# A first score block that takes the high and low halves of K in one matmul, an output projection moved behind the third score block, and a later split of the Q weights

## The chip, the cores and the metric

The kernel runs on one core of one Trainium2 chip. A core has five engines that run side by side and wait for each other through semaphores: TensorE (PE in the profile, with its weight loads as PEld), VectorE (DVE), ScalarE (ACT), GpSimd (POOL) and SyncE (SP), which here issues the DMAs. The metric is the device time of one execution in microseconds (us); lower is better. All times below are in us unless marked ns.

## What is computed

Two transformer layers on `x` of shape (2, 512, 256), all in float32. The change lies in the attention of the second layer, which the reference writes as (cut):

```
def _L1_attn_ref(x, W_Q, W_K, W_V, W_O, b_Q, b_K, b_V, b_O):
    q = jnp.einsum('bpd,hde->bphe', x, W_Q) + b_Q
    k = jnp.einsum('bpd,hde->bphe', x, W_K) + b_K
    v = jnp.einsum('bpd,hde->bphe', x, W_V) + b_V
    scores = jnp.einsum('bqhe,bkhe->bhqk', q, k) / ATTN_SCALE
    scores = jnp.where(causal, scores, IGNORE)
    attn = jax.nn.softmax(scores, axis=-1)
    z = jnp.einsum('bkhe,bhqk->bqhe', v, attn)
    out = jnp.einsum('bqhe,hed->bqd', z, W_O) + b_O
```

There are 16 heads of 128 channels and two halves of the batch with 512 positions each, so 32 pairs of a head and a half. Ahead of it stand a first attention (3 heads) and a feed-forward part with ternary weights; behind it an int8 product.

## The kernel before

**Windows.** Each pair of a head and a half is one *window*, `w` = 0 to 31. The heads go two by two (a *pair* of heads shares one set of weights `W_hi`, `W_lo`), and a pair of heads serves four windows. The kernel is a software pipeline: while window `w` is on the engines, its instructions belong to neighbours. TensorE computes the scores of window `w+1`, the projections Q, K, V of window `w+2`, the weighted values of window `w-1` and the output projection of an older one.

**High and low parts.** Every float32 operand is split into a high part and a remainder (`Q_hi`, `Q_lo`, ...), and each product is three matmuls into the same PSUM bank: high by high, high by low, low by high (`split_mm`, lines 389 to 391). For the scores these are lines 673 to 675. ScalarE makes the high part out of PSUM, VectorE the low part.

**The order is written by hand.** For each engine there is a table of steps per window, a letter and a number each. Those that matter here:

- `S0` to `S3`: the scores of window `w+1`, query block 0 to 3 of 128 rows. Causal, so block `c` needs `128*(c+1)` keys, and its matmuls have that many columns. On VectorE `S` is `max1` (line 1435): one custom instruction adds the causal mask to the scores, writes them to `SM` and leaves the row's extreme in `nmax`. On ScalarE it is the exponential (line 924) into `PR`.
- `Q0`, `K1`, `V2`: projections of window `w+2`. They use the PSUM banks 0 and 1 in turn, so each waits until VectorE has read the one before last: `K1` waits for `V_lo` of window `w+1` (VectorE's step `W2`, line 1422), `V2` waits for `Q_lo` (VectorE's step `Q0`, line 1425), and the scores `S0` of the next window wait for `K_lo`.
- `O0`: half of an output projection, 12 matmuls of 256 columns on TensorE; on VectorE the addition of the result to `X` (line 1475). `B0`: the weighted values of window `w-1`. `Z0`: the low part of an earlier `Z`.
- `U0` to `U3`: VectorE turns the probabilities in blocks (line 1454) into `BT`; SyncE stores `BT` to DRAM and loads it back turned as `MV`; ScalarE (`C3` to `C0`, line 935) and GpSimd (`moved_low`, line 1112) split `MV` into `PT_hi` and `PT_lo`, which `B0` one window later needs. Windows 0 to 25 go this way (`by_dma`); later ones are turned by TensorE.
- `G0` to `G3`: VectorE splits the next pair's weights, when `loads_k(w)` or `loads_o(w)` say so. `G0` is `W_Q` in two instructions, `W_hi` (line 1361) and `W_lo` (line 1363); `G1` and `G2` are the high parts of `W_K` and `W_V` (line 1365), whose low parts GpSimd makes; `G3` is `W_O`. `G0` to `G2` run in windows 1, 5, 9, 13, 17, 21 and 23 only.
- `R0`, `R1`: reciprocals of the row sums; GpSimd then scales `PR` (lines 1096 to 1105).

In a window below 26 each query block has a PSUM bank of its own (`s_bank`: `bank[2 + c]`), so block 0 uses 128 of its bank's 512 columns.

Of the kernel before, what the change touches and what calls it, by code (L numbers as in the profile page):

```python
# [23 lines left out]
P = 128  # L24
# [3 lines left out]
SEQ = 512  # L28
# [32 lines left out]
def build(nc, x, wq0, wk0, wv0, fcT, fcb, wupT, wgateT, wdownT, pack1, bias_all, bo1, qw, qb, out):  # L61
    ctx = ExitStack()
    with ctx:
        def sb(name, shape, dt=F32, where=ctx):
            return where.enter_context(nc.sbuf_tensor(name, shape, dt))

        def sem(name):
            return ctx.enter_context(nc.semaphore(name))
# [9 lines left out]
        causal = sb("causal", [P, SEQ])  # L78
# [70 lines left out]

        Q_hi = sb("Q_hi", [P, 2, SEQ], F32R)  # L150
        Q_lo = sb("Q_lo", [P, 2, SEQ], F32R)
        K_hi = sb("K_hi", [P, 2, SEQ], F32R)
        K_lo = sb("K_lo", [P, 2, SEQ], F32R)
        V_hi = sb("V_hi", [P, V_GROUPS * CT, 2 * DH], F32R)
        V_lo = sb("V_lo", [P, V_GROUPS * CT, 2 * DH], F32R)
        SM = sb("SM", [P, 2, SEQ])
        PR = sb("PR", [P, CT, SEQ])
        PT_hi = [sb(f"PT_hi{i}", [P, CT, SEQ], F32R) for i in range(2)]
        PT_lo = [sb(f"PT_lo{i}", [P, CT, SEQ], F32R) for i in range(2)]
# [61 lines left out]
        pj_psum, pj_hi, pj_lo = sem("pj_psum"), sem("pj_hi"), sem("pj_lo")  # L221
        s_psum, s_max, s_exp, s_rec, p_norm = (sem(n) for n in ("s_psum", "s_max", "s_exp", "s_rec", "p_norm"))
        t_psum, pt_hi, t_free = sem("t_psum"), sem("pt_hi"), sem("t_free")
        bt_done = sem("bt_done")
        stored = [sem(f"stored{i}") for i in range(2)]
        moved = [sem(f"moved{i}") for i in range(2)]
        mv_hi, mv_lo = sem("mv_hi"), sem("mv_lo")
# [17 lines left out]
        def steps(text):  # L245
            return [(step[0], int(step[1])) for step in text.split()]

        FIRST_MOVED, LAST_MOVED = 0, WINDOWS - 7
        STEADY_PE = (steps("S0 Q0 S1 O0 S2 K1 S3 V2 B0"),
                     steps("S0 Q0 S1 O0 S2 K1 S3 V2 B0"))  # L250
        STEADY_ACT = (steps("S0 C3 C2 Q0 S1 C1 C0 S2 K1 S3 V2 B0"),
                      steps("S0 C3 C2 Q0 S1 C1 C0 S2 K1 S3 V2 B0"))
        STEADY_DVE = (steps("S0 Z0 U2 U3 W2 S1 Q0 S2 O0 G0 G1 G2 G3 R0 S3 K1 U0 U1 R1"),
                      steps("S0 Z0 U2 U3 W2 S1 G0 Q0 S2 O0 G1 G3 R0 S3 K1 G2 U0 U1 R1"))
        EVEN_PE = steps("T0 T1 S0 O0 T2 T3 S1 Q0 S2 O1 K1 A0 S3 V2")
        EVEN_ACT = steps("T0 T1 W2 S0 T2 T3 S1 Q0 S2 K1 A0 S3")
        EVEN_DVE = steps("T0 T1 S0 W2 O0 T2 T3 S1 Q0 S2 O1 R0 K1 S3 A0 R1")
# [2 lines left out]

        PE_ORDER = {w: STEADY_PE[w % 2] for w in range(1, LAST_MOVED + 1)} | {
            0: steps("S0 S1 Q0 S2 K1 S3 V2"),
# [13 lines left out]
            WINDOWS - 2: steps("T0 T1 S0 S1 T2 S2 T3 W2 S3"),  # L276
            WINDOWS - 1: steps("T0 T1 B0 T2 A0 T3 A1 X0 I0 I1")}
        DVE_ORDER = {w: STEADY_DVE[w % 2] for w in range(1, LAST_MOVED)} | {
            1: steps("S0 Z0 U2 U3 W2 S1 G0 Q0 S2 O0 G1 G3 R0 S3 K1 G2 U0 U1 R1"),
            0: steps("U2 W2 S0 U3 S1 Q0 S2 R0 S3 K1 U0 U1 R1"),  # L280
            LAST_MOVED: steps("S0 Z0 U2 U3 W2 S1 G0 Q0 S2 O0 G1 G3 R0 S3 K1 G2 R1"),
            WINDOWS - 6: steps("S0 Z0 W2 T0 T1 O0 S1 G3 T2 Q0 S2 T3 R0 K1 B0 S3 R1 A0"),
            WINDOWS - 5: EVEN_DVE,
            WINDOWS - 4: steps("T0 T1 S0 W2 O0 T2 T3 S1 L0 Q0 S2 O1 L1 R0 K1 S3 A0 R1 L2"),
# [27 lines left out]
        def s_bank(w, c):  # L312

            return bank[2 + c] if by_dma(w) else bank[2 + c % 2]

        def by_dma(w):

            return FIRST_MOVED <= w <= LAST_MOVED
# [48 lines left out]
        def pj0_bank(use):  # L367
            return bank[3 + use % 3]
# [99 lines left out]
        def _(pe):  # L468
# [14 lines left out]
            for g in range(GF_USES):  # L483
# [11 lines left out]
                dst = pj0_bank(g)  # L495
# [165 lines left out]
            def scores(w, c):  # L661

                slot = w % 2
                if c == 0:
                    pe.wait_ge(pj_lo, 3 * w + 2)
                if w == 0 and c == 2:
                    pe.wait_ge(prod_done, FFN_STEPS)
                if w > 0:
                    pe.wait_ge(s_max, 4 * w + c - (3 if by_dma(w) else 1))
                n = (c + 1) * P  # L670
                dst = s_bank(w, c)
                cols = slice(c * P, (c + 1) * P)
# [138 lines left out]
        def _(act):  # L811
# [212 lines left out]
        def _(pool):  # L1024
# [67 lines left out]
            def normalise(w, part):  # L1092

                pool.wait_ge(s_rec, 2 * w + part + 1)
                if part == 0:
                    pool.tensor_tensor(PR[:, 0, 0:P], PR[:, 0, 0:P], rec1[:, 0:1].to_broadcast([P, P]),  # L1096
                                       ALU.mult).then_inc(p_norm, 1)
                    for c in range(1, CT - 1):
                        pool.tensor_scalar(PR[:, c, 0:(c + 1) * P], PR[:, c, 0:(c + 1) * P], rec1[:, c:c + 1], 1.0,
                                           ALU.mult, ALU.mult).then_inc(p_norm, 1)  # L1100
                else:

                    pool.tensor_tensor(PR[:, CT - 1, 0:P], PR[:, CT - 1, 0:P],
                                       rec1[:, CT - 1:CT].to_broadcast([P, P]), ALU.mult)
                    pool.tensor_scalar(PR[:, CT - 1, P:SEQ], PR[:, CT - 1, P:SEQ], rec1[:, CT - 1:CT], 1.0,
                                       ALU.mult, ALU.mult).then_inc(p_norm, 1)
# [45 lines left out]
        def _(dve):  # L1152
# [276 lines left out]
            def max1(w, c):  # L1429
                dve.wait_ge(masks, 1)  # L1430
                dve.wait_ge(s_psum, 4 * w + c + 1)
                if not (isinstance(w, int) and w == 0 and c < 2):
                    dve.wait_ge(s_exp, 4 * w + c - 1)
                n = (c + 1) * P
                dve.tensor_tensor_reduce(SM[:, c % 2, 0:n], s_bank(w, c)[:, 0:n], causal[:, SEQ - n:SEQ], 1.0,  # L1435
                                         HIGHEST, ALU.add, ALU.min, nmax1[:, c:c + 1]).then_inc(s_max, 1)

            def recip1(w, part):
# [41 lines left out]
            for t in (CT, CT + 1):  # L1480
                dve.scalar_tensor_tensor(X[:, t, :], bank[6][:, (t - CT) * D:(t - CT + 1) * D], gdscale[:, 0:1],
                                         X[:, t, :], ALU.mult, ALU.add).then_inc(x_added, 1)
            max1(0, 0)
            max1(0, 1)
            dve.wait_ge(x_added, CT * 2 * HALVES - 2)
            ln_statistics(5, 0, 2)
# [172 lines left out]
```

## Time and profile before

| | |
|---|---|
| median of 3 runs | 516.11 us (515.94 to 516.92) |
| the profiled execution: its time | 516.04 us |
| its span in the profile | 514.3 us |
| granted TensorE clock, mean over the span | 0.989 of 2.4 GHz |

The profiled execution is one run on the chip; its span runs from its first to its last instruction, and what is above the span lies around it. A row of the timeline gives the start, the duration, engine, line of the kernel, operation, output and inputs, and in brackets how long the engine had been idle before and what ended that. Ends of matmuls are modelled, so for TensorE starts are compared with starts. Where a row says `128x256`, 128 is the partitions and 256 the elements in each (for a matmul its columns).

### The profile page before, as it was taken

What the parts mean: (1) busy time and instruction counts of PE and PEld (TensorE: products, weight loads), DVE (VectorE), ACT (ScalarE), POOL (GpSimd) and SP (SyncE); (2) the same over time, 40 slices, a digit from 0 to 9 for tenths busy, and PEclk for the clock granted to TensorE, in tenths of its full rate; (3) what the DMA queues carried; (4) which work ended last, traced back from release to release, by engine and by line L of the source; (5) the groups of instructions that cost most, each with busy time, mean ns of one, the idle gap of its engine ahead of it and who ended that gap; (6) DMA issues with size and microseconds to landing.
All of it is one profiled execution on the core that took longest, in us unless ns stands there. A gap on an engine that the chain in (4) does not pass through costs nothing.

```text
span 514.3 us, 8933 instructions
## 1 busy us (share of the span) xinstructions
PE 488.5 (95%) x3042; PEld 434.6 (85%) x3042; DVE 385.8 (75%) x943; ACT 295.4 (57%) x690; POOL 285.4 (55%) x379
## 2 busy tenths in 40 slices
PE   8999999999999978999999999999999999999962
PEld 7888999899888867898998998998998889899851
DVE  3666886765756579779779779779779886678897
ACT  2356426535455556766676767756766666655552
POOL 1345134422756458776686777767777794512344
PEclk9999999999999999999999999999999999999995
DMA  9900000000010017664664664664654654000002
GB/s 281 370 16 2 1 0 1 1 0 1 24 41 1 0 55 192 196 168 129 196 169 129 196 172 125 195 172 126 196 170 133 190 151 126 3 1 0 1 1 83
DMA packets 54365, 51.60 MB, mean 100 GB/s; under 512 B 3504, under 2 KB 49712, under 8 KB 54320
## 3 DMA queue, kind: packets, MB, share of 16 engines
q1 hardware_dynamic: 53232, 49.98, 34.3%
q10 hardware_dynamic: 1088, 1.05, 0.6%
q8 instruction: 25, 0.41, 0.3%
q14 instruction: 20, 0.16, 0.1%
HBM read 32.92 MB, written 18.09 MB: 99 GB/s over the span
## 4 chain that ended last, share of the span: by engine, by line
PE 72%; DVE 14%; ACT 4%; issue 4%; DMA 3%; POOL 2%; SPq 1%; DVEq 0%; ACTq 0%
PE bank L389 18%; PE bank L390 17%; PE bank L391 17%; PE bank L609 3%; PE bank L610 3%; PE bank L673 3%; PE bank L674 3%; PE bank L675 3%; DVE SM L1435 2%; DMA Wv_sb<-wv 2%; PE bank L620 2%; PE bank L622 1%; DVE BT L1454 1%; ACT PR L924 1%; DVE XN L1169 1%
## 5 line engine op out<-in xcount | busy, mean ns | idle before, releaser
L1112 POOL TENSOR_TENSOR PT_lo<-MV,PT_hi 128x512 fp32r<-128x512 f32 (+1 forms) x104 | 92.9, 924 | 48.2 <-ACT PT_hi L935 48.0
L924 ACT ACTIVATE PR<-SM,nmax 128x128 f32<-128x128 f32 (+3 forms) x128 | 72.1, 563 | 68.7 <-DVE nmax L1435 66.2
L1435 DVE CUSTOM_DVE_ANT_0 SM<-bank,causal 128x128 f32<-128x128 f32 (+3 forms) x128 | 61.5, 481 | 34.2 <-issue 24.3
L1057 POOL TENSOR_TENSOR E_lo<-E,E_hi 128x512 fp32r<-128x512 f32 x24 | 31.1, 1300 | 55.0 <-ACT E_hi L848 47.4
L389 PE MATMUL bank<-XT_hi,W_hi 128*128 128x512 f32 x128 | 52.3, 409 | 3.8 <-DVE V_lo L1422 2.5
L1454 DVE STREAM_TRANSPOSE BT<-PR 128x128 f32<-128x128 f32 (+1 forms) x104 | 48.2, 492 | 5.2 <-POOL PR L1096 3.1
L935 ACT CAST PT_hi<-MV 128x512 fp32r<-128x512 f32 (+1 forms) x104 | 42.2, 454 | 14.8 <-DMA MV<-turned_dram 14.5
L390 PE MATMUL bank<-XT_lo,W_hi 128*128 128x512 f32 x128 | 50.4, 394 | 0.0
L391 PE MATMUL bank<-XT_hi,W_lo 128*128 128x512 f32 x128 | 50.4, 394 | 0.0
L673 PE MATMUL bank<-K_hi,Q_hi 128*128 128x128 f32 (+3 forms) x128 | 42.0, 328 | 1.1 <-DVE K_lo L1425 1.1
L390 PE MATMUL bank<-PT_lo,V_hi 128*128 128x128 f32 (+3 forms) x130 | 41.6, 320 | 0.0
L391 PE MATMUL bank<-PT_hi,V_lo 128*128 128x128 f32 (+3 forms) x130 | 41.6, 320 | 0.0
L674 PE MATMUL bank<-K_lo,Q_hi 128*128 128x128 f32 (+3 forms) x128 | 41.3, 322 | 0.0
L675 PE MATMUL bank<-K_hi,Q_lo 128*128 128x128 f32 (+3 forms) x128 | 41.3, 322 | 0.0
L843 ACT ACTIVATE E<-bank,nmax 128x512 f32<-128x512 f32 x24 | 16.5, 688 | 42.3 <-DVE nmax L1242 42.2
L389 PE MATMUL bank<-PT_hi,V_hi 128*128 128x128 f32 (+3 forms) x130 | 40.2, 309 | 0.5 <-POOL PT_lo L1112 0.3
L389 PE MATMUL bank<-W_hi,XT_hi 128*128 128x256 f32 x128 | 36.5, 285 | 3.9 <-DVE Q_lo L1425 3.9
L389 PE MATMUL bank<-WO_hi,Z_hi 128*128 128x256 f32 x128 | 36.1, 282 | 1.9 <-DVE Z_lo L1469 1.9
L390 PE MATMUL bank<-WO_lo,Z_hi 128*128 128x256 f32 x128 | 35.8, 280 | 0.0
L391 PE MATMUL bank<-W_hi,XT_lo 128*128 128x256 f32 x128 | 35.8, 280 | 0.0
L390 PE MATMUL bank<-W_lo,XT_hi 128*128 128x256 f32 x128 | 35.8, 280 | 0.0
L391 PE MATMUL bank<-WO_hi,Z_lo 128*128 128x256 f32 x128 | 35.6, 278 | 0.0
(171 smaller groups left out, 1571.1 us busy)
## 6 DMA issues: line engine op xcount, KB each, us to landing
MV<-turned_dram SPq DMA_DIRECT2D x104, 160.0 KB, 3.3
turned_dram<-BT SPq DMA_DIRECT2D x26, 384.0 KB, 2.9
stage<-pack SPq DMA_DIRECT2D x32, 256.0 KB, 3.9
turned_dram<-BT SPq DMA_DIRECT2D x26, 256.0 KB, 3.3
X<-x SPq DMA_DIRECT2D x2, 512.0 KB, 8.7
wraw<-wupT SPq DMA_DIRECT2D x1, 1024.0 KB, 9.7
wraw<-wgateT SPq DMA_DIRECT2D x1, 1024.0 KB, 11.5
wraw<-wdownT SPq DMA_DIRECT2D x1, 1024.0 KB, 13.8
```

The source lines that it names most:

```text
L389: pe.matmul(dst, a_hi, b_hi, start=first, stop=False, skip_group_check=share)
L390: pe.matmul(dst, a_hi, b_lo, start=False, stop=False, skip_group_check=share)
L391: return pe.matmul(dst, a_lo, b_hi, start=False, stop=last, skip_group_check=share)
L673: pe.matmul(dst[:, 0:n], Q_hi[:, slot, cols], K_hi[:, slot, 0:n], start=True, stop=False)
L674: pe.matmul(dst[:, 0:n], Q_hi[:, slot, cols], K_lo[:, slot, 0:n], start=False, stop=False)
L675: pe.matmul(dst[:, 0:n], Q_lo[:, slot, cols], K_hi[:, slot, 0:n], start=False, stop=True).then_inc(s_psum, 1)
L924: act.activation(PR[:, c, 0:(c + 1) * P], SM[:, c % 2, 0:(c + 1) * P], ACT.Exp, bias=nmax1[:, c:c + 1], scale=-1.0, accum_out=sum1[:, c:c ...
L935: act.copy(by_quad(PT_hi[w % 2], c), moved_part(w, c)).then_inc(mv_hi, 1)
L1057: pool.tensor_tensor(E0_lo[:, m, :], E0[:, m, :], E0_hi[:, m, :], ALU.subtract).then_inc(e0_lo, 1)
L1112: pool.tensor_tensor(by_quad(PT_lo[w % 2], c), moved_part(w, c), by_quad(PT_hi[w % 2], c), ALU.subtract).then_inc(mv_lo, 1)
L1435: dve.tensor_tensor_reduce(SM[:, c % 2, 0:n], s_bank(w, c)[:, 0:n], causal[:, SEQ - n:SEQ], 1.0, HIGHEST, ALU.add, ALU.min, nmax1[:, c:c + ...
L1454: dve.transpose(BT[w % 2][:, :, moved_blocks(c), :].rearrange("p j b c -> p b j c"), PR[:, c, 0:(c + 1) * P].rearrange("p (b j c) -> p b j ...
```

## The change

`K_hi` and `K_lo` become two slices of one tile `K_parts`, side by side. For the first query block of a window that goes by DMA (scores of windows 0 to 25), one matmul takes `Q_hi` against 128 columns of `K_hi` and 128 of `K_lo`, 256 columns in all, into columns 0 to 255 of the bank; a second adds `Q_lo` by `K_hi` to columns 0 to 127. VectorE adds columns 128 to 255 and the mask into a new tile `SB`, waits on its own semaphore `s_low` for that, and then runs the custom instruction with `SB` in place of the mask. In windows 1 to 25 TensorE's `O0` goes behind `S2`. In odd windows VectorE's `G0` goes from behind `S1` to behind `O0`. In window 25 some steps are struck that did nothing there.

```diff
@@ tiles @@
-        K_hi = sb("K_hi", [P, 2, SEQ], F32R)
-        K_lo = sb("K_lo", [P, 2, SEQ], F32R)
+        K_parts = sb("K_parts", [P, 2, 2, SEQ], F32R)
+        K_hi, K_lo = K_parts[:, :, 0, :], K_parts[:, :, 1, :]
+        SB = sb("SB", [P, P])
@@ order of the steps: TensorE, both parities @@
-        STEADY_PE = (steps("S0 Q0 S1 O0 S2 K1 S3 V2 B0"),
+        STEADY_PE = (steps("S0 Q0 S1 S2 O0 K1 S3 V2 B0"),
@@ order of the steps: VectorE, odd windows @@
-                      steps("S0 Z0 U2 U3 W2 S1 G0 Q0 S2 O0 G1 G3 R0 S3 K1 G2 U0 U1 R1"))
+                      steps("S0 Z0 U2 U3 W2 S1 Q0 S2 O0 G0 G1 G3 R0 S3 K1 G2 U0 U1 R1"))
@@ scores on TensorE @@
+                if c == 0 and by_dma(w):
+
+                    pe.matmul(dst[:, 0:2 * P].rearrange("p (a k) -> p a k", a=2), Q_hi[:, slot, cols],
+                              K_parts[:, slot, :, 0:P], start=True, stop=False, skip_group_check=True)
+                    pe.matmul(dst[:, 0:P], Q_lo[:, slot, cols], K_hi[:, slot, 0:P], start=False, stop=True,
+                              skip_group_check=True).then_inc(s_psum, 1)
+                    return
@@ max1 on VectorE @@
-                dve.tensor_tensor_reduce(SM[:, c % 2, 0:n], s_bank(w, c)[:, 0:n], causal[:, SEQ - n:SEQ], 1.0,
+                mask = causal[:, SEQ - n:SEQ]
+                if c == 0 and by_dma(w):
+                    mask = SB[:]
+                    dve.tensor_tensor(mask, s_bank(w, c)[:, P:2 * P], causal[:, SEQ - n:SEQ], ALU.add).then_inc(s_low, 1)
+                    dve.wait_ge(s_low, w + 1)
+                dve.tensor_tensor_reduce(SM[:, c % 2, 0:n], s_bank(w, c)[:, 0:n], mask, 1.0,
                                          HIGHEST, ALU.add, ALU.min, nmax1[:, c:c + 1]).then_inc(s_max, 1)
```

On VectorE in window 9, one of the windows with a weight split, the stretch from `S1` to `S3` reads before (`ISA SM` is `max1`'s custom instruction, `ISA nmax` its second half, `X<-bank,X` the step `O0`, `CAST W_hi` the step `G1`):

```order
L1435 ISA SM,nmax<-bank,causal 128x256
L1435 ISA nmax 128x1
L1361 TENSOR_SCALAR W_hi<-stage 128x512
L1363 SCALAR_TENSOR_TENSOR W_lo<-stage,W_hi 128x512
L1425 SCALAR_TENSOR_TENSOR Q_lo<-bank,bias,Q_hi 128x512
L1435 ISA SM,nmax<-bank,causal 128x384
L1435 ISA nmax 128x1
L1475 TENSOR_TENSOR X<-bank,X 128x512
L1365 CAST W_hi<-stage 128x512
L1442 RECIPROCAL rec<-sum 128x3
```

and with the change (its lines are numbered some 8 to 13 higher):

```order
L1448 ISA SM,nmax<-bank,causal 128x256
L1448 ISA nmax 128x1
L1433 SCALAR_TENSOR_TENSOR Q_lo<-bank,bias,Q_hi 128x512
L1448 ISA SM,nmax<-bank,causal 128x384
L1448 ISA nmax 128x1
L1488 TENSOR_TENSOR X<-bank,X 128x512
L1369 TENSOR_SCALAR W_hi<-stage 128x512
L1371 SCALAR_TENSOR_TENSOR W_lo<-stage,W_hi 128x512
L1373 CAST W_hi<-stage 128x512
L1455 RECIPROCAL rec<-sum 128x3
```

The two instructions of `G0` now stand behind `Q_lo`, the third block's maximum and the addition to `X`; what follows `G1` is in the same order as before.

Where VectorE passes from window 9 to window 10, from `U1` over the first block's maximum to `V_lo`, the change reads:

```order
L1467 STREAM_TRANSPOSE BT<-PR 128x2x4x32
L1455 RECIPROCAL rec<-sum 128x1
L1446 TENSOR_TENSOR SB<-bank,causal 128x128
L1448 ISA SM,nmax<-bank,SB 128x128
L1448 ISA nmax 128x1
L1474 SCALAR_TENSOR_TENSOR Z_lo<-bank,bias,Z_hi 128x512
L1467 STREAM_TRANSPOSE BT<-PR 128x3x4x32
L1467 STREAM_TRANSPOSE BT<-PR 128x4x4x32
L1430 TENSOR_TENSOR V_lo<-bank,V_hi 128x512
```

The row `TENSOR_TENSOR SB` is new; before, the custom instruction followed the reciprocal directly, with `causal` as its second input.

## Rows read from the trace of the kernel before

**Rows 1.** The page, part 1: busy time, share of the span, instructions.

```profile
PE 488.5 (95%) x3042; PEld 434.6 (85%) x3042; DVE 385.8 (75%) x943; ACT 295.4 (57%) x690; POOL 285.4 (55%) x379
```

**Rows 2.** Windows view (length; busy PE, PEld, DVE, ACT, POOL): window 8; 9-10; 21-22.

```profile
260.49:269.83 9.34, 9.34 (x62) 8.56 (x62) 7.49 (x21) 6.55 (x16) 7.31 (x13) 1.00 0.60 163
269.83:289.35 19.52, 19.00 (x122) 17.12 (x122) 16.66 (x42) 12.85 (x32) 14.78 (x21) 1.00 0.55 148
385.29:404.30 19.01, 19.01 (x122) 17.18 (x122) 16.11 (x42) 12.85 (x32) 14.84 (x21) 1.00 0.59 158
```

**Rows 3.** Waits, 210 to 434 us: total, times, longest.

```profile
ACT PT_hi L935 <- DMA MV<-turned_dram: 11.7, 13, 2.2
...
PE bank L389 <- DVE Q_lo L1425: 2.4, 5, 0.5
```

**Rows 4.** Timeline, three engines: weight splits of windows 9 and 21.

```profile
272.12 4.03 POOL L1112 TENSOR_TENSOR PT_lo<-MV,PT_hi 128x512 fp32r<-128x512 f32 x4 [2.21 <-ACT PT_hi L935]
273.42 1.26 DVE L1361 TENSOR_SCALAR W_hi<-stage 128x512 fp32r<-128x512 f32 x1
274.72 1.11 DVE L1363 SCALAR_TENSOR_TENSOR W_lo<-stage,W_hi 128x512 fp32r<-128x512 f32 x1
275.75 0.74 DVE L1425 SCALAR_TENSOR_TENSOR Q_lo<-bank,bias,Q_hi 128x512 fp32r<-128x512 f32 x1
276.63 0.36 PE L389 MATMUL bank<-W_hi,XT_hi 128*128 128x256 f32 x1 [0.52 <-DVE Q_lo L1425]
277.49 0.41 DVE L1365 CAST W_hi<-stage 128x512 fp32r<-128x512 f32 x1
283.30 3.38 POOL L1112 TENSOR_TENSOR PT_lo<-MV,PT_hi 128x512 fp32r<-128x512 f32 x4 [0.16 <-ACT PT_hi L935]
388.89 0.42 DVE L1361 TENSOR_SCALAR W_hi<-stage 128x512 fp32r<-128x512 f32 x1
```

**Rows 5.** TensorE's timeline in window 9: first rows of S0, Q0, S1, O0.

```profile
269.83 0.28 PE L673 MATMUL bank<-K_hi,Q_hi 128*128 128x128 f32 x1
270.17 0.44 PE L389 MATMUL bank<-XT_hi,W_hi 128*128 128x512 f32 x1
271.62 0.28 PE L673 MATMUL bank<-K_hi,Q_hi 128*128 128x256 f32 x1
271.97 0.29 PE L389 MATMUL bank<-WO_hi,Z_hi 128*128 128x256 f32 x1
```

**Rows 6.** VectorE by line and form: names, shapes, count, busy, mean ns.

```profile
L1446 DVE TENSOR_TENSOR PT_lo<-bank,PT_hi 128x128 fp32r<-128x128 f32 x6 | 1.7, 282 | 0.0
```

**Rows 7.** Timeline of window 8: V_lo on VectorE, K1 on TensorE.

```profile
263.16 0.65 DVE L1422 TENSOR_TENSOR V_lo<-bank,V_hi 128x512 fp32r<-128x512 f32 x1
264.53 0.39 PE L389 MATMUL bank<-XT_hi,W_hi 128*128 128x512 f32 x1
```

**Rows 8.** The same two places in window 10.

```profile
282.69 0.65 DVE L1422 TENSOR_TENSOR V_lo<-bank,V_hi 128x512 fp32r<-128x512 f32 x1
283.99 0.39 PE L389 MATMUL bank<-XT_hi,W_hi 128*128 128x512 f32 x1
```

**Rows 9.** Timeline of the opening, windows 1 and 2, three engines.

```profile
197.17 0.42 DVE L1361 TENSOR_SCALAR W_hi<-stage 128x512 fp32r<-128x512 f32 x1
197.52 0.68 ACT L918 ACTIVATE Q_hi<-bank,bias 128x512 fp32r<-128x512 f32 x1
199.22 0.74 DVE L1425 SCALAR_TENSOR_TENSOR Q_lo<-bank,bias,Q_hi 128x512 fp32r<-128x512 f32 x1
201.98 0.75 DVE L1425 SCALAR_TENSOR_TENSOR K_lo<-bank,bias,K_hi 128x512 fp32r<-128x512 f32 x1
206.96 0.47 PE L389 MATMUL bank<-XT_hi,W_hi 128*128 128x512 f32 x1 [0.66 <-DVE V_lo L1422]
```

**Rows 10.** Timeline of window 7: C3 on ScalarE, B0 on TensorE.

```profile
254.20 1.03 ACT L935 CAST PT_hi<-MV 128x512 fp32r<-128x512 f32 x2 [1.92 <-DMA MV<-turned_dram]
258.53 0.50 PE L389 MATMUL bank<-PT_hi,V_hi 128*128 128x512 f32 x1
```

More of the change, by code:

```diff
@@ L223, in build @@
         t_psum, pt_hi, t_free = sem("t_psum"), sem("pt_hi"), sem("t_free")
-        bt_done = sem("bt_done")
+        s_low, bt_done = sem("s_low"), sem("bt_done")
         stored = [sem(f"stored{i}") for i in range(2)]
@@ L248, in build @@
         FIRST_MOVED, LAST_MOVED = 0, WINDOWS - 7
-        STEADY_PE = (steps("S0 Q0 S1 O0 S2 K1 S3 V2 B0"),
-                     steps("S0 Q0 S1 O0 S2 K1 S3 V2 B0"))
+        STEADY_PE = (steps("S0 Q0 S1 S2 O0 K1 S3 V2 B0"),
+                     steps("S0 Q0 S1 S2 O0 K1 S3 V2 B0"))
         STEADY_ACT = (steps("S0 C3 C2 Q0 S1 C1 C0 S2 K1 S3 V2 B0"),
@@ L278, in build @@
         DVE_ORDER = {w: STEADY_DVE[w % 2] for w in range(1, LAST_MOVED)} | {
-            1: steps("S0 Z0 U2 U3 W2 S1 G0 Q0 S2 O0 G1 G3 R0 S3 K1 G2 U0 U1 R1"),
+            1: steps("S0 Z0 U2 U3 W2 S1 Q0 S2 O0 G0 G1 G3 R0 S3 K1 G2 U0 U1 R1"),
             0: steps("U2 W2 S0 U3 S1 Q0 S2 R0 S3 K1 U0 U1 R1"),
-            LAST_MOVED: steps("S0 Z0 U2 U3 W2 S1 G0 Q0 S2 O0 G1 G3 R0 S3 K1 G2 R1"),
+            LAST_MOVED: steps("S0 Z0 U2 U3 W2 S1 Q0 S2 O0 R0 S3 K1 R1"),
             WINDOWS - 6: steps("S0 Z0 W2 T0 T1 O0 S1 G3 T2 Q0 S2 T3 R0 K1 B0 S3 R1 A0"),
```

## Prediction

> **What bounds it now.** I read the page's busy shares first: TensorE works for 488.5 of 514.3 us, 95%, and VectorE for 75% [rows 1]. That is an average, so the windows come next [rows 2]. In window 8, without a weight split, TensorE is busy for the whole 9.34: only fewer or shorter matmuls help there. Windows 9 and 10 last 19.52 with 19.00 of TensorE work, windows 21 and 22 the same work in 19.01. Those .52 are what the split costs where it falls badly. The list of waits names them: between 210 and 434 us TensorE's projections wait five times for `Q_lo`, 2.4 in all, and ScalarE waits 13 times for `MV` to land from DRAM, 11.7 in all [rows 3]. The split's own rows show why the pairs differ [rows 4]: `W_hi` took .42 in window 21 but 1.26 in window 9, while GpSimd's `PT_lo` was running (272.12 to 276.15). `Q_lo` stands behind it, and `V2` behind `Q_lo`.
>
> The profiled execution took 516.04, within .07 of the median of 516.11; the sum below starts from 516.04. About .2%, 1.03 us, is what can be told from no change.
>
> **Term 1: TensorE's first scores.** In window 9 the three matmuls of 128 columns take from 269.83 to 270.17, .34; three of 256 columns take from 271.62 to 271.97, .35 [rows 5]. So a matmul of 256 columns costs .117 and one of 128 .113: here the count sets the price, not the columns. Two instead of three save .34 − .23 = .11 per window. The trace has no matmul with its columns in two slices. It may cost up to twice a 128-column one (columns 384 before and after: saving 0); .17 is the most, if only half the time is left. Scores 0 to 25 have the new form, but the saving reaches the end only where TensorE is the bound and stays it. That is in the ten windows without a split beside them, 3, 4, 7, 8, 11, 12, 15, 16, 19 and 20: **−1.1** (0 to −1.7).
>
> The Trainium skill speaks against this term: "TensorE: Matmul & The Clock Gate", Back-to-back issue gap, gives an isolated gap of N/2.4 + 2.5 ns, so about 56 ns at 128 columns and 109 at 256. By that, 167 ns become 165 and nothing is saved. The trace disagrees in both sizes, .113 and .117.
>
> **Term 2: VectorE's new addition.** No row has it. The nearest is a subtraction of 128x128 out of PSUM with a mean of .282 [rows 6]; rows overlap, and its step to the next is about .21. The custom instruction needs the sum, so it can't overlap it. In window 9 `W_lo`, which needs `W_hi`, starts .04 after `W_hi` ends, while `Q_lo`, which needs nothing of `W_lo`, starts .08 before `W_lo` ends [rows 4]: .12 for the dependence. I take .21 + .12 = **.33**. Bounds: .2 with no cost of waiting, .77 if it were as dear as a 512-column subtraction at .65 [rows 7] plus .12. About half of term 1's .11 lets it start sooner, so what is queued behind, above all `V_lo`, comes .27 later.
>
> Who waits for that is `K1`. In window 8 `V_lo` ends at 263.81 and `K1` starts at 264.53 [rows 7]. `Q_lo` of window 9 ends at 276.49, and the matmul it releases starts at 276.63 [rows 4]: .14 for the signal. So `V_lo` has .58 to spare. The addition takes .27, the earlier `K1` .11: .20 is left, and the plain windows pay nothing. From an addition of about .53 on they would.
>
> **Term 3: `O0` behind `S2`.** TensorE's work is the same. `O0` is 12 matmuls at .117, 1.4, and `S2` comes that much earlier; three matmuls of 384 columns at the same rate put `O0` some .53 later, so it ends near 273.9 in window 9. VectorE's addition to `X` comes behind `Q_lo`, at 276 or later [rows 4], and doesn't notice. `S2` is not what VectorE waits for before `Q_lo`. Cover is over 2 us on either side: **0**.
>
> **Term 4: `G0` behind the addition to `X`.** Window 9 before: `W_hi` starts at 273.42, `Q_lo` at 275.75, `G1` at 277.49 [rows 4]. So `G0` took 2.33 and `Q_lo` to `X` 1.74. Undisturbed, `G0` would be **1.49**: `W_hi` at window 21's .42, the gap of .04, and `W_lo`'s step to `Q_lo`, 1.03. Now `Q_lo` starts at 273.42 + .27 = 273.69, `V2` doesn't wait any more, and `G0` starts at 275.43. `PT_lo` takes 3.38 when less disturbed (its row at 283.30), so GpSimd is done at about 275.5 to 275.8 and `G0` is nearly free of it: it ends at 276.92, .57 earlier than before.
>
> What is late next: window 10's `V_lo`. It started at 282.69 [rows 8]; −.57 and the second addition's +.33 make 282.45, it ends at 283.10 and releases `K1` at 283.24, which before started at 283.99. TensorE alone, with two plain windows of 9.23, would be there at 283.00. So the pair gives .75, of which I take **.7** (bounds: .4 if `PT_lo` still blocks `G0` for .34; 1.06 for 19.52 − 2 × 9.23). There are four such pairs, 5/6, 9/10, 13/14 and 17/18: **−2.8**. Pair 21/22, at 19.01 [rows 2], goes to the same 18.8: **−.2**. In windows 23 and 24 `W_O` is split as well and VectorE stays the bound: **0** (at most −.7).
>
> The Trainium skill, "SBUF — State Buffer", Who interferes with whom, says that VectorE in a two-port mode, or with two inputs in SBUF, and GpSimd shut each other out for a whole instruction. The trace agrees, with `W_hi` at 1.26 against .42; rival B is what the rule would do to the moved `G0` if `PT_lo` isn't over.
>
> **Term 5: the opening, windows 0 to 2.** Here VectorE has no slack: `K1` of window 2 waits .66 for `V_lo` [rows 9]. Two additions lie on its chain, one not fully: +.17 + .33 = +.5. In window 1 `G0` filled the time until ScalarE's `Q_hi` was there: it started at 197.17, `Q_lo` at 199.22, but `Q_hi` ended at 198.20. With `G0` gone from there, `Q_lo` starts when `Q_hi` allows, near 198.7 with the .5. The distance `Q_lo` to `K_lo` was 2.76 (199.22 to 201.98), and `G0` now lies inside it. `PT_lo` starts late here (`G0` took 2.05 beside it), so I give it 1.8, between 1.49 and 2.33: `K_lo` at 203.26 instead of 201.98, +1.3. The third addition and the saving of one matmul bring `K1` of window 2 from 206.96 to 208.5: **+1.5** (bounds +.85, with 1.49 and half of the shift; +2.1 with 2.33).
>
> **Term 6: late landings.** Windows that become shorter leave `MV` less time. In window 7 ScalarE waited 1.92 for `MV`, and `B0` started at 258.53 only, behind it and GpSimd [rows 10]. Such a landing does not come earlier because TensorE does. The 13 waits of [rows 3] fall on about half of the windows; in three plain ones `B0` was late, or nearly. What terms 1 and 4 gain ahead of such a landing is given back: **+.7** (0 to +1.4, a third of terms 1 and 4).
>
> **Sum.** −1.1 + 0 + 0 − 2.8 − .2 + 1.5 + .7 = −1.9; 516.04 − 1.9 = **514.1**. All terms at their good bounds give about 511, all at their bad ones about 519.5.
>
> **Rivals.** *A: columns set the price.* Term 1 is 0, the rest stands: 515.2, no change that could be told. Against it are the two equal prices [rows 5]; for it only that the sliced operand has no row. 10%. (It is where the Trainium skill's formula in "TensorE: Matmul & The Clock Gate", Back-to-back issue gap, would lead.)
>
> *B, the other sign: the moved `G0` is shut out by `PT_lo` at its new place too.* If `MV` lands later or `S1` comes earlier, `G0` still takes 2.33. Then window 10's `V_lo` comes at 282.69 + .27 + .33 and the four pairs cost +.1 each, pair 21/22 +.6 and the opening 2.1: −1.1 + .4 + .6 + 2.1 = +2.0, **518.0**. Each .1 on `G0` costs .4 in the pairs and .1 each in 21/22 and the opening, so from 1.49 upwards the gain of 1.9 is gone at about 1.8. For it: 1.26 in window 9. Against: GpSimd's end at 276.15 lies only .7 behind the new start. 13%.
>
> *C: the opening and the landings eat it.* Term 5 at +2.1 and term 6 at +1.4: 515.4, no change that could be told. For it: both are waits that the change does nothing about. 15%.
>
> *D: no landing in the way*, and an opening of +.85: −1.1 − 2.8 − .2 + .85 = −3.2, 512.8. For it: in most windows `B0` had time to spare. 20%.
>
> **Numbers.** The forecast, 514.1, has 42%. Forecast and D are faster: 62%. A and C are the same: 25%. B is slower: 13%. The range of 512.2 to 516.9 leaves out B and the lower edge of D, some 18%; the forecast's own is 513 to 515.
>
> **What would show it.** First score to first projection on TensorE in window 9: .23 right, .34 rival A. Plain windows at 9.23. `V2` no longer waits for `Q_lo`, and `W_hi` behind the addition to `X` takes .42; near 1.2 there is rival B. The pairs last 18.8. The step from the new `SB` row to the custom instruction is .33; above .53, waits of `K1` for `V_lo` appear in plain windows. `K1` of window 2 stands at 208.5. Waits of `B0` for `PT_lo` grow by no more than .7 in all. The forecast is wrong if the opening costs over 2, or if a wait that isn't named here, of `K1` for `V_lo` above all, stands in every window.

## The result, and the profile after

The changed kernel takes 512.31 us, the median of 6 runs (511.3 to 513.17), against 516.03 of 6 runs of the kernel before (515.61 to 518.7): a ratio of 0.9927, 95% interval 0.991 to 0.9943. It is 3.7 us faster; the forecast was 1.9 (514.1), in a range of 512.2 to 516.9, so the time lies .1 inside the range's lower end. The profiled execution took 512.32, its span is 510.5, and TensorE's granted clock was 0.99 as before.

The page's busy shares are those of before [rows 1] less 26 matmuls, plus 26 instructions of VectorE:

```profile
PE 485.2 (95%) x3016; PEld 432.3 (85%) x3016; DVE 383.0 (75%) x969; ACT 294.2 (58%) x690; POOL 282.9 (55%) x379
```

The windows view answers to [rows 2] (length, then busy PE, PEld, DVE, ACT, POOL). Its rows are windows 0 to 2 of the kernel before, then of the changed kernel windows 0 to 2, window 8, windows 9 and 10, windows 21 and 22:

```profile
182.74:212.41 29.67, 23.87 (x133) 19.76 (x133) 23.96 (x65) 18.76 (x47) 23.96 (x35) 1.00 0.53 145
182.85:213.66 30.81, 23.81 (x130) 19.48 (x130) 23.70 (x68) 18.57 (x47) 23.69 (x35) 1.00 0.50 139
260.60:270.45 9.85, 9.74 (x61) 8.44 (x61) 7.18 (x20) 6.36 (x16) 5.61 (x10) 1.00 0.83 220
270.45:288.99 18.54, 18.54 (x121) 16.92 (x120) 16.08 (x44) 12.84 (x32) 15.10 (x22) 1.00 0.53 149
383.01:401.70 18.69, 18.69 (x121) 17.10 (x120) 15.99 (x44) 12.87 (x32) 15.15 (x22) 1.00 0.54 151
```

In windows 9 and 10 TensorE is now busy for all of 18.54, where .52 of 19.52 were lost. Windows 0 to 2 took 29.67 before and take 30.81. Window 8 was 9.34 and is 9.85, with TensorE waiting. In the waits view, 211 to 431 us (total, times, longest), against [rows 3], the row of TensorE behind `Q_lo` is gone, and ScalarE waits more for landings:

```profile
ACT PT_hi L943 <- DMA MV<-turned_dram: 15.7, 17, 2.2
PEld bank L390 <- POOL W_lo L1076: 1.2, 1, 1.2
PE bank L390 <- DVE V_lo L1430: 1.0, 1, 1.0
```

The last two are one stall, in window 24. (In windows 8 and 20 `V2` still starts .26 and .36 late, behind a `Q_lo` that itself stands behind a late landing; the waits view has no row for it.) The timeline of window 9 shows every step of the change; it answers to [rows 4] and [rows 5]. First `S0` and `Q0` on TensorE, then VectorE's addition, `Q_lo` and `G0`, the last piece of `PT_lo` on GpSimd, and `V2`:

```profile
270.45 0.33 PE L676 MATMUL bank<-K_parts,Q_hi 128*128 128x256 f32 x1
270.63 0.23 PE L678 MATMUL bank<-K_parts,Q_lo 128*128 128x128 f32 x1
270.69 0.44 PE L390 MATMUL bank<-XT_hi,W_hi 128*128 128x512 f32 x1
270.94 0.29 DVE L1446 TENSOR_TENSOR SB<-bank,causal 128x128 f32<-128x128 f32 x1 [0.86 <-issue]
271.27 0.29 DVE L1448 CUSTOM_DVE_ANT_0 SM<-bank,SB 128x128 f32<-128x128 f32 x1
274.15 0.75 DVE L1433 SCALAR_TENSOR_TENSOR Q_lo<-bank,bias,Q_hi 128x512 fp32r<-128x512 f32 x1
275.89 0.42 DVE L1369 TENSOR_SCALAR W_hi<-stage 128x512 fp32r<-128x512 f32 x1
275.94 0.69 POOL L1120 TENSOR_TENSOR PT_lo<-MV,PT_hi 128x128 fp32r<-128x128 f32 x1
276.34 0.84 DVE L1371 SCALAR_TENSOR_TENSOR W_lo<-stage,W_hi 128x512 fp32r<-128x512 f32 x1
276.48 0.28 PE L390 MATMUL bank<-W_hi,XT_hi 128*128 128x256 f32 x1
277.10 0.41 DVE L1373 CAST W_hi<-stage 128x512 fp32r<-128x512 f32 x1
```

`S0` to `Q0` is .24 instead of .34. The step from `SB` to the custom instruction is .33. `V2` starts without a wait, 2.3 after `Q_lo`. `G0` takes 275.89 to 277.10, 1.21 instead of 2.33.

Where the time went, by the starts of `S0` in both traces (S0 to S0, after less before): windows 0 to 2 +1.14; the pairs 5/6, 9/10, 13/14 and 17/18 (a window with a weight split and the one behind it) −.50, −.98, −.83 and −.97; 21/22 −.32; 23/24 −.61; the ten plain windows together −.25; window 26 −.54. Of the plain ones, those with nothing late in either trace save some .10 each (9.34 to 9.24, 9.46 to 9.36), while 8, 12 and 20 became .2 to .5 longer and 7 and 16 some .45 shorter. The kernel before has only this one trace, and its span of 514.3 is a long one: its 61 timed runs beside the experiments have a median span of 513.5, and 47 of them are below 514.3.

### The profile page after: what moved, and what is told of

It is laid out like the page before. It is cut to its first block, busy times and chain, and to the rows that moved or that the text cites. A ratio compares the mean times of both kernels' runs of the same rounds, so it can differ in the third digit from the quotient of the medians.

```text
span 510.5 us, 8907 instructions
## 1 busy us (share of the span) xinstructions
PE 485.2 (95%) x3016; PEld 432.3 (85%) x3016; DVE 383.0 (75%) x969; ACT 294.2 (58%) x690; POOL 282.9 (55%) x379
## 4 chain that ended last, share of the span: by engine, by line
PE 76%; DVE 11%; DMA 5%; ACT 3%; POOL 2%; issue 2%; SPq 1%; DVEq 0%; ACTq 0%
PE bank L390 19%; PE bank L392 18%; PE bank L391 18%; PE bank L610 3%; PE bank L611 3%; PE bank L682 2%; PE bank L683 2%; PE bank L681 2%; DMA Wv_sb<-wv 2%; DMA MV<-turned_dram 2%; PE bank L621 2%; PE bank L623 2%; DMA turned_dram<-BT 1%; DVE SM L1448 1%; DVE BT L1467 1%
## 5 line engine op out<-in xcount | busy, mean ns | idle before, releaser
L1120 POOL TENSOR_TENSOR PT_lo<-MV,PT_hi 128x512 fp32r<-128x512 f32 (+1 forms) x104 | 91.3, 909 | 51.5 <-ACT PT_hi L943 51.2
L1448 DVE CUSTOM_DVE_ANT_0 SM<-bank,causal 128x384 f32<-128x384 f32 (+3 forms) x102 | 54.0, 530 | 9.3 <-PE bank L683 6.7
L1433 DVE SCALAR_TENSOR_TENSOR Q_lo<-bank,bias,Q_hi 128x512 fp32r<-128x512 f32 x32 | 24.0, 750 | 15.1 <-ACT Q_hi L926 14.9
L949 ACT ACTIVATE Z_hi<-bank,bias 128x512 fp32r<-128x512 f32 x31 | 21.3, 688 | 23.6 <-PE bank L392 23.6
L681 PE MATMUL bank<-K_parts,Q_hi 128*128 128x384 f32 (+3 forms) x102 | 34.8, 342 | 0.0
```

Source lines behind the costliest of these rows:

```text
L949: act.activation(Z_hi[g % 2][:, h, :], bank[6][:], ACT.Identity, bias=bias1[:, p, 4 + h:5 + h], scale=1.0).then_inc(z_hi, 1)
L1120: pool.tensor_tensor(by_quad(PT_lo[w % 2], c), moved_part(w, c), by_quad(PT_hi[w % 2], c), ALU.subtract).then_inc(mv_lo, 1)
L1433: ins = dve.scalar_tensor_tensor(lo[:, w % 2, :], src, bias1[:, p, 2 * which + h:2 * which + h + 1], hi[:, w % 2, :], ALU.add, ALU.subtract)
```

## The experiments

Each run was timed beside the kernel before, whose own medians lay between 514.8 and 516.2, so the ratios are what is compared. The changed kernel has 0.9927. The span is the median over the timed runs, and the last column is the median of what the time lies above the span.

| run | median us | ratio (95%) | span | above it |
|---|---|---|---|---|
| *kernel before, beside the next four* | 515.75 | | 513.4 | 2.5 |
| new scores alone | 515.96 | 1.0004 (0.9988 to 1.0020) | 514.15 | 1.8 |
| G0 back | 516.57 | 1.0012 (0.9997 to 1.0026) | 514.75 | 1.8 |
| O0 back | 512.16 | 0.9932 (0.9914 to 0.9951) | 510.35 | 1.8 |
| orders alone | 513.71 | 0.9956 (0.9940 to 0.9972) | 510.8 | 2.7 |
| *kernel before, beside the next four* | 516.23 | | 513.65 | 2.5 |
| opening as before | 512.14 | 0.9923 (0.9897 to 0.9950) | 510.3 | 1.8 |
| three matmuls | 514.70 | 0.9974 (0.9957 to 0.9991) | 512.15 | 2.5 |
| Q0 ahead of C3 | 513.97 | 0.9961 (0.9943 to 0.9980) | 512.1 | 1.8 |
| small reloads | 511.17 | 0.9904 (0.9881 to 0.9926) | 509.35 | 1.8 |
| *kernel before, beside the next four* | 514.80 | | 512.7 | 2.0 |
| addition twice | 512.18 | 0.9950 (0.9930 to 0.9969) | 510.35 | 1.8 |
| addition four times | 522.25 | 1.0139 (1.0115 to 1.0162) | 520.4 | 1.8 |
| old scores for the first 3 | 511.49 | 0.9928 (0.9909 to 0.9947) | 509.65 | 1.8 |
| the same, W_O later | 511.68 | 0.9934 (0.9912 to 0.9957) | 509.85 | 1.8 |

**Time outside the span.** The last column falls into two groups. Where the first block is two matmuls, in all windows to 25 or from scores 3 on, the time lies 1.8 or 1.9 above the span in all 83 runs, those of the changed kernel among them. With three in every window (the kernel before, orders alone, three matmuls) it lies 1.7 to 3.1 above, with medians of 2.0 to 2.7. So some .2 to .9 of what separates the two groups arises outside the span, where no view shows it. It goes with the count of TensorE instructions (3016 or 3019 against 3042) and not with that of all instructions (the addition four times has the most, 8985). Its cause stays open. Below, what a matmul costs in the windows is read from spans and rows, not from times.

**New scores alone.** The new first block, with both orders as before:

```diff
-        STEADY_PE: S0 Q0 S1 S2 O0 K1 S3 V2 B0
+        STEADY_PE: S0 Q0 S1 O0 S2 K1 S3 V2 B0
-        odd windows, VectorE: ... S1 Q0 S2 O0 G0 G1 ...
+        odd windows, VectorE: ... S1 G0 Q0 S2 O0 G1 ...
```

> Only the new form of the first score block; O0 and G0 stand where they stood before. Theory (the move of G0 makes nearly all of the gain): the plain windows save .11 each, some 1 us in all, the opening loses .5, the pairs with a weight split stay at 19.5 because VectorE still reaches Q_lo late; 516 us, between 515 and 517, no change that can be told. Rival (the saved matmuls make the gain, .11 to .12 in each of 26 windows): 513.0. In the trace the theory wants TensorE to wait some .6 for Q_lo in windows 5, 9, 13, 17, 23; the rival wants window lengths of 9.24 to 9.35 there.

515.96: nothing gained, as the theory had it; the span is .75 longer than before. Its timeline of window 9 has `W_hi` blocked and `V2` waiting as before:

```profile
274.49 1.25 DVE L1369 TENSOR_SCALAR W_hi<-stage 128x512 fp32r<-128x512 f32 x1
276.81 0.74 DVE L1433 SCALAR_TENSOR_TENSOR Q_lo<-bank,bias,Q_hi 128x512 fp32r<-128x512 f32 x1
277.70 0.36 PE L390 MATMUL bank<-W_hi,XT_hi 128*128 128x256 f32 x1 [0.64 <-DVE Q_lo L1433]
```

**G0 back.** Only VectorE's lines of the diff above, on the changed kernel:

> The changed kernel with G0 alone put back behind S1. Theory: loses the gain of the pairs (about .5 to 1 us each, five pairs and 23/24), wins back .75 of the opening: 515.5 to 516.5. Rival (saved matmuls make the gain): 512.5 to 513. If O0's move does something by itself, this run and the one with the new scores alone differ by more than 1 us; the theory wants them equal.

516.57, just above what was expected: the whole gain is gone, and the span is 1.35 longer than before. The two runs without `G0`'s move agree within their intervals, with `O0` in either place.

**O0 back.** Only TensorE's line:

> The changed kernel with TensorE's O0 put back ahead of S2. Theory (the move of O0 is worth nothing): 512.3, within .8 of the changed kernel. Rival (S2's earlier scores are what lets VectorE run through Q_lo, S2 and X ahead of G0 without a wait): G0 starts later by up to 1.4 in the split windows, and TensorE waits for K_lo or V_lo behind it; 513.5 to 515.

512.16, the changed kernel's time. Its trace has a small price that I had not looked for. With the addition ahead of it on VectorE, `Z_lo` ends at 272.51, close to the start of `O0` at its old place, and in odd windows `O0` needs it. That this is a wait for `Z_lo` is inferred, since the waits view has no row for it. The step from its first matmul to its second is .19 and not .11, in the odd windows only:

```profile
272.76 0.36 PE L390 MATMUL bank<-WO_hi,Z_hi 128*128 128x256 f32 x1
272.95 0.28 PE L391 MATMUL bank<-WO_lo,Z_hi 128*128 128x256 f32 x1
273.07 0.28 PE L392 MATMUL bank<-WO_hi,Z_lo 128*128 128x256 f32 x1
```

That is .08 in some ten windows, too little for this measurement.

**Orders alone.** Both moves, with the old scores:

```diff
-                if c == 0 and by_dma(w):
+                if False:
```

> The changed kernel with the old three matmuls and no addition in the first score block; O0 and G0 stand as in the changed kernel. Theory: the pairs last 18.8 to 18.9 instead of 18.5 to 18.7, plain windows 9.34 to 9.45 as before, the opening loses .75 instead of 1.1; 514.0, between 513.3 and 514.7. Rival (saved matmuls make the gain): 515.5 or more.

513.71, three fifths of the gain in time. In the span it is nearly all of it: 510.8 against 513.4 before, where the changed kernel has 510.5 and O0 back 510.35. The opening loses .40 and not the expected .75. Its windows 0 to 2, 9 and 10, and 21 and 22:

```profile
182.99:213.06 30.07, 24.06 (x133) 19.77 (x133) 23.20 (x65) 18.58 (x47) 23.77 (x35) 1.00 0.52 143
269.69:288.44 18.75, 18.75 (x123) 17.13 (x122) 15.66 (x42) 13.13 (x32) 15.11 (x22) 1.00 0.57 155
382.79:401.70 18.91, 18.91 (x123) 17.32 (x122) 15.74 (x42) 12.96 (x32) 14.50 (x21) 1.00 0.57 156
```

The pairs are TensorE's already; the new scores then take another .2 from each, and .1 from most other windows. In the two traces the changed kernel gives that back in the opening (.74), in windows 6, 8, 12 and 20 with their late landings (.2 to .5 each) and in window 24 (.42).

**Three matmuls.** The first block's halves side by side as in the change, but by three matmuls:

```diff
-                    pe.matmul(dst[:, 0:2 * P]..., Q_hi[:, slot, cols], K_parts[:, slot, :, 0:P], ...)
+                    pe.matmul(dst[:, 0:P], Q_hi[:, slot, cols], K_hi[:, slot, 0:P], ...)
+                    pe.matmul(dst[:, P:2 * P], Q_hi[:, slot, cols], K_lo[:, slot, 0:P], ...)
```

> The changed kernel, but the first score block is made by three matmuls of 128 columns, high by high into columns 0 to 127, high by low into 128 to 255, low by high onto 0 to 127; VectorE's addition stays, so only the count of matmuls differs. Theory (the number of matmuls sets the price, .11 each, in each of some 22 windows that TensorE bounds): 514.7, S0 to Q0 at .34 and windows of 9.35 to 9.46. Rival (the price goes by columns, 384 in both; the gain is the orders'): 512.3, S0 to Q0 as in the changed kernel.

514.70, 2.4 above the changed kernel and on the theory's figure, but in part by luck: only 1.65 of it is in the span (512.15 against 510.5), the rest outside. The columns are 384 in both kernels, so the count pays: windows without a late landing take 9.34 to 9.47, .1 more each. TensorE's rows in window 9, and windows 9 and 10 (18.75 against 18.54):

```profile
270.62 0.28 PE L676 MATMUL bank<-K_parts,Q_hi 128*128 128x128 f32 x1
270.74 0.28 PE L678 MATMUL bank<-K_parts,Q_hi 128*128 128x128 f32 x1
270.85 0.28 PE L680 MATMUL bank<-K_parts,Q_lo 128*128 128x128 f32 x1
270.96 0.44 PE L390 MATMUL bank<-XT_hi,W_hi 128*128 128x512 f32 x1
```

```profile
270.62:289.37 18.75, 18.75 (x122) 17.13 (x122) 16.07 (x44) 12.81 (x32) 15.15 (x22) 1.00 0.53 151
```

**The addition twice and four times.** Copies of the addition into a tile that nothing reads (three tiles for the second run):

```diff
+                    dve.tensor_tensor(SB2[:], s_bank(w, c)[:, P:2 * P], causal[:, SEQ - n:SEQ], ALU.add)
                     dve.wait_ge(s_low, w + 1)
```

> The changed kernel with VectorE's addition done a second time into a tile that nothing reads, ahead of the wait: VectorE's chain behind the first block gets one more step, about .21. Theory (in the changed kernel V_lo ends .36 before it would hold back K1, so a step of .21 is covered in every window but 0 to 2 and 24): 512.3 + .2 to .7 = 512.5 to 513.0, K1 at the same 3.92 to 3.98 into its window. Rival (VectorE's chain is paid for in every window): 512.3 + 26 x .21 = 517.8.

> The same with three additions more, some .63. Theory (beyond .36 the rest is paid for once a window): V_lo ends at 4.06, K1 starts at 4.20 instead of 3.92 to 3.98, .25 in each of some 20 windows, and .6 in each of windows 0 to 2 and 24: 512.3 + 5 + 2.4 = 519.7, between 518 and 521. Rival (paid in every window, from the first step on): 528.7. Rival (VectorE has more room than that): 513 to 515.

Twice: ratio 0.9950, some 1.2 us above the changed kernel, with overlapping intervals, and the same span (510.35 against 510.5). `K1` stays at 3.92 to 3.97 into the plain windows, as the theory wanted; the rival's 5 us are out. VectorE's rows in window 15 of this run show that the copy costs .07 and not .21, since it fills the time in which the custom instruction waited for the sum (`SB` to `SM` is .40, against .33):

```profile
326.41 0.29 DVE L1447 TENSOR_TENSOR SB<-bank,causal 128x128 f32<-128x128 f32 x1 [1.52 <-issue]
326.62 0.28 DVE L1448 TENSOR_TENSOR SB<-bank,causal 128x128 f32<-128x128 f32 x1
326.81 0.28 DVE L1450 CUSTOM_DVE_ANT_0 SM<-bank,SB 128x128 f32<-128x128 f32 x1
```

Four times: 522.25, ratio 1.0139, more than expected. `V_lo` ends 3.89 into a plain window and `K1` starts at 4.04, .06 to .12 late, less than I had worked out; `V2` then starts up to .19 late and `B0` likewise, and plain windows take 9.43 to 9.49. The rest came from the windows behind a split, where `K1` starts at 4.39 to 4.44, from late landings (10.56 at the longest), from window 24 (11.44) and from 0 to 2 (32.58). So the room behind `V_lo` is real and is used up between one and three copies.

**The opening.** The old scores for scores 0, 1 and 2; then that with `G0` of window 1 back as well:

```diff
-                if c == 0 and by_dma(w):
+                if c == 0 and by_dma(w) and w >= 3:
```

> The changed kernel with the old three matmuls and no addition for scores 0, 1 and 2 only. Theory (the opening has no room for the addition; from window 3 on it has): windows 0 to 2 take 30.1 instead of 30.8, 511.6. Rival (the first landing of MV, which B0 of window 1 waits for, sets the opening's length): 30.8 as before, 512.3.

> The changed kernel with the old three matmuls and no addition for scores 0, 1 and 2, and with G0 of window 1 alone back behind S1; all later windows as changed. Theory (VectorE's chain in windows 0 to 2 pays for both): windows 0 to 2 take 29.7 to 29.9 again instead of 30.8, and the time is 511.2, 1.0 to 1.1 under the changed kernel. Rival (the opening's loss is TensorE's waiting for something else, or is regained later): 512.3.

The first gave 511.49, ratio 0.9928; windows 0 to 2 take 30.12 (its row below), as expected, .7 less than in the changed kernel, but windows 8, 10, 12 and 16 were long by late landings and the time can't be told from the changed kernel's. The second gave 512.14 and did not show its 29.7: in the execution profiled `MV` landed 4.0 into window 1, `B0` stood until 8.29, and the three windows took 30.72. Windows 0 and 2 are .75 shorter than in the changed kernel, window 1 is .66 longer. The theory holds for the first run's trace; the second leaves open what `G0` of window 1 costs by itself.

```profile
182.54:212.66 30.12, 23.75 (x133) 19.75 (x132) 23.48 (x66) 18.58 (x47) 23.72 (x35) 1.00 0.52 142
```

**Late landings.** Two runs. ScalarE's `Q0` put ahead of `C3` and `C2`:

```diff
-        STEADY_ACT: S0 C3 C2 Q0 S1 C1 C0 S2 K1 S3 V2 B0
+        STEADY_ACT: S0 Q0 C3 C2 S1 C1 C0 S2 K1 S3 V2 B0
```

> The changed kernel with ScalarE's step Q0 ahead of C3 and C2 in windows 2 to 25, so that Q_hi doesn't stand behind the wait for MV. Theory (a late landing costs at two places: C3 holds back Q_hi and V2, and B0 waits for the split): V2's waits of .3 in the two windows with the latest landings go, B0's stay, 511.8. Rival (C3 behind Q_hi makes the split later in every window): B0 waits in most windows, 514 to 517.

513.97, at the rival's lower edge, but not by its way: `B0` starts where it did in most windows. `V2`'s waits for a late `Q_hi` are gone, as the theory had it. What cost most of the time is rival B of the prediction, made to happen: `C3` now starts at 2.46 in windows without a late landing, and so GpSimd's `PT_lo` runs later. `G0` meets it at its new place, and `W_hi` takes .97 to .99 in windows 5, 9, 13, 17, 21 and 23. Here window 9:

```profile
276.06 0.75 POOL L1120 TENSOR_TENSOR PT_lo<-MV,PT_hi 128x256 fp32r<-128x256 f32 x1
276.12 0.98 DVE L1369 TENSOR_SCALAR W_hi<-stage 128x512 fp32r<-128x512 f32 x1
277.14 0.83 DVE L1371 SCALAR_TENSOR_TENSOR W_lo<-stage,W_hi 128x512 fp32r<-128x512 f32 x1
```

The windows behind them, 6, 10, 14, 18 and 22, are 9.53 to 9.87, with `K1` waiting for `V_lo`. (The longest, window 7 at 10.63, has the latest landing of this trace, with `C3` at 4.37.)

And the reloads of the weights cut down, from the second pair of heads on, which keeps the first pair's weights in most of the staging tile and so leaves that part of the computation out (what the edit comes to):

```diff
-                cols = slice(part * W_COLS, (part + 1) * W_COLS)
+                cols = slice(part * W_COLS, part * W_COLS + 16)
```

> The changed kernel with the reloads of the attention weights from the second pair of heads on cut to 16 of 512 columns (8 of 256 KB each); the rest of the staging tile keeps the first pair's weights, so the output is not the reference's. Theory (the weight loads, queued between one window's MV and the next one's store, make the landing late): no C3 later than 3 us into its window, B0's waits in windows 6 to 20 gone, 510.7. Rival (the path by DRAM varies by itself): as many late landings as in the changed kernel, 512.3.

511.17, ratio 0.9904: the size that the theory gave, but not its picture. `C3` still starts 3.2 to 3.5 into windows 5, 10, 12, 18 and 20; only landings beyond 3.5, of which the changed kernel has four, are gone. That the loads lengthen the latest landings is not shown by it: with full loads, orders alone has none beyond 3.5 either, and the addition twice has one from window 3 on. Something else spreads them.

**W_O later.** On the first of the two opening kernels, GpSimd's low part of `W_O` in window 23 behind its scaling of `PR`:

```diff
+                if loads_o(w) and not loads_k(w):
                     split_b(loads_o(w))
                 normalise(w + 1, 0)
                 normalise(w + 1, 1)
+                if loads_o(w) and loads_k(w):
+                    split_b(loads_o(w))
```

> The run before with one thing more: in window 23, the only one that splits W_Q, W_K, W_V and W_O together, GpSimd makes W_O's low part (1.29) behind its scaling of PR and not ahead of it. Theory (window 24's wait of 1.2 for V_lo comes from VectorE standing before PR there): window 24 shrinks from 10.56 to 9.4 or 9.6, 510.5. Rival (VectorE's own work holds window 24 back): 511.6, window 24 as it was.

Window 24 went from 10.62 to 9.98 (9.4 to 9.6 expected), since `K1` starts 4.04 into it and not 5.16; `B0` now waits there for `PT_lo`, which has the late `W_O` ahead of it. The time, 511.68, is within the noise of the changed kernel's. None of the versions is measurably faster than the changed kernel.

## Why the prediction was right, step by step

**Right in sign and in its cause, lucky in the range.** The change is faster, and `G0` does it: the changed kernel without `G0`'s move is no faster than before, and the two moves without the new scores are. The size is off: 3.7 is twice the 1.9, and the time is nearer to rival D's 512.8 (20%) than to the forecast, but D's condition did not hold, since windows 6, 8, 12 and 20 had late landings. Part of the gain lies outside the span, some .2 to .7 by the table, and no term had it.

**Term 4, the pairs: right mechanism, too small.** Forecast −2.8, −.2 and 0; measured −3.28, −.32 and −.61. The mis-sized step is `G0` itself: 1.49 forecast, 1.21 measured, since `W_lo` took a step of .76. It also began .16 earlier in its window than forecast (5.44, not 5.60), since `Q_lo` did. Two of the four pairs came close to the bound given, and in 9/10 and 17/18 TensorE has no wait left; 5/6 has a late landing in window 6. Windows 23 and 24, priced at nothing, gained in 23 (10.13 to 9.24) and gave .28 back in 24.

What I had put wrongly is why `W_hi` took 1.26 in window 9 and .42 in window 21. I read it as `PT_lo` running or not. It was running in both; what differs is which began first. GpSimd's rows in the kernel before, one piece of `PT_lo` in each window, beside `W_hi` at 273.42 and 388.89 [rows 4]:

```profile
273.39 1.01 POOL L1112 TENSOR_TENSOR PT_lo<-MV,PT_hi 128x384 fp32r<-128x384 f32 x1
388.92 1.26 POOL L1112 TENSOR_TENSOR PT_lo<-MV,PT_hi 128x384 fp32r<-128x384 f32 x1
```

In window 9 the piece began .03 ahead, and `W_hi` lost .84; in window 21 `W_hi` began .03 ahead, and the piece lost .25. In windows 5, 13, 17 and 23 of that trace `W_hi` began while a piece was running and took .91 to 1.21: it ended .28 or .29 behind that piece each time. In the changed kernel `W_hi` begins .05 ahead of the last piece (275.89 and 275.94), and in the run with `Q0` ahead of `C3` it begins .06 behind one. That is how the Trainium skill tells it in "SBUF — State Buffer", Who interferes with whom: whoever issues first has the shared ports for the whole instruction. The forecast's reason, that `PT_lo` would be over by 275.5 to 275.8, did not come true: it ended at 276.63. `W_hi` came first by .05, as it did by .05 or .06 in windows 5, 13, 17 and 21.

**Rival B** was therefore closer than it looked, but not at its price of 2.33. Had `W_hi` begun behind that last piece, it would have waited for no more than the piece's .46 (what it takes at 285.62 in the same trace, with nothing in its way), which by my estimate makes `G0` 1.4 to 1.6. To lose more, GpSimd must be later. In the run with `Q0` ahead of `C3`, `W_hi` begins 5.44 into window 9 as in the changed kernel, but GpSimd's third piece begins at 5.38 and not at 4.80, and `G0` takes 1.77. Even there, windows 17 and 18 took 18.96, against 18.53 in the changed kernel and 19.50 before: `V2` is free of `Q_lo` in any case, and part of the gain remains.

**Term 1: the price right, its reach too small.** .10 per window, from the starts of `S0` and `Q0` (.24 against .34). The prediction counted ten windows; the run with three matmuls has it in all of windows 3 to 23 without a late landing, because the pairs are now TensorE's too (there it stood inside term 4's bound). In the spans it is 1.65. Rival A is out by that run. The formula of the Trainium skill, "TensorE: Matmul & The Clock Gate", Back-to-back issue gap, gives an estimate of 165 ns for the two matmuls and 167 for the three; the rows have 240 and 340.

**Term 2: right.** The step is .33 as forecast. `V_lo` ends at 3.43 into a plain window, .10 later than before and not .27, because, in window 9, VectorE begins .15 earlier and the step to `Z_lo` lost a gap of .07; the room is .36 and not .20.

**Term 3: 0, right,** but for the reason of no use: had `O0` stayed, odd windows would have cost .08, it seems by way of `Z_lo`. I asked what the move costs and not what staying would.

**Term 5: +1.5 forecast, +1.14 measured; the mis-sized part is `G0`.** In the forecast the first two additions make .5, the third less the saved matmul .2, and so `G0` .8. The two moves alone make windows 0 to 2 30.07, +.40, and without the additions there the changed kernel has 30.12, so that the additions make .69, as forecast, and the moves some .4 to .45. In the changed kernel `G0` of window 1 took 1.52 (200.13 to 201.65), where 1.8 was given.

**Term 6: +.7 forecast.** Terms 1 and 6 together were −.4 on the plain windows; measured −.25. Where a landing is late the place is as described, and there is one more link: ScalarE's `C3` waits 2.09 in window 8, `Q_hi` stands behind it, `V2` behind `Q_lo`, and then `B0`:

```profile
264.33 1.03 ACT L943 CAST PT_hi<-MV 128x512 fp32r<-128x512 f32 x2 [2.09 <-DMA MV<-turned_dram]
265.99 0.75 DVE L1433 SCALAR_TENSOR_TENSOR Q_lo<-bank,bias,Q_hi 128x512 fp32r<-128x512 f32 x1 [1.61 <-ACT Q_hi L926]
266.88 0.36 PE L390 MATMUL bank<-W_hi,XT_hi 128*128 128x256 f32 x1
268.48 0.50 PE L390 MATMUL bank<-PT_hi,V_hi 128*128 128x512 f32 x1
```

Which windows are hit differs: 7 and 16 before, 6, 8, 12 and 20 after, none beyond .1 us with the orders alone. What makes a landing late is not settled.

**Not foreseen: window 26**, −.54. It is most likely no effect of the change. `C3` starts 2.78 into it before, behind a late landing, and 1.74 after. The window is 12.77 to 12.79 in all other traces, also in those without the moves and without the new scores; but of the kernel before there is only the one.

So, between the two traces, the forecast's sum was short by 1.8: .6 on pairs 5/6 to 21/22, .6 on 23/24, .5 in window 26, .4 in the opening, less .15 on the plain windows and .1 that lies ahead of window 0. The typical span shrank by less than these traces do (510.5 against medians of 512.7 to 513.65), and the rest of the 3.7 came from outside it. The bounds, too, were added wrongly: as the terms state them they make some 510 and 517.7, not 511 and 519.5.

## What to carry to other kernels

Where a helper engine's result stands in the queue ahead of what the bound engine waits for, look at moving it behind first: here that was worth more than shortening the bound engine's work, and the shortening then paid in more places. When an instruction's duration differs between two places, look at the neighbour's start to the hundredth: who was first may be all that differs. Where it is first by .05 us only, work out what being second would cost, here the rest of one short piece. Price a moved step also by what it would cost left where it was. Compare spans as well as times: a difference in time that the span does not have is not explained by any row.

## What the hardware showed that was not expected

- VectorE's `W_hi` (512 elements, .42 alone) and GpSimd's subtraction shut each other out by a start .03 us ahead: 1.26 and 1.01 us one way round, .42 and 1.26 the other.
- An independent instruction of .29 put between an addition and the custom instruction that waits for it cost .07, since the wait of some .12 was there anyway.
- One matmul of 256 columns in two slices 512 columns apart and one of 128 take .24 together; three of 128 take .34.
- With 26 or 23 matmuls fewer, the time above the span fell from medians of 2.0 to 2.7 (1.7 to 3.1) to 1.8 or 1.9 in each of 83 runs. Nothing here shows why.
- `C3`, which waits for the landing of `MV` through DRAM, started anywhere between 1.4 and 4.5 us into its window over these traces.
